# LayerNorm + causal attention + ternary FFN on eight cores: one constant to another queue, an earlier wait for the constants, and part of a 3.5 MB reload moved from SyncE's queue to GpSimd's

## What is computed

```python
xn = layernorm(x)
q = rope((xn @ wq).reshape(B, S, 16, 128));  k = rope(xn @ wk ...);  v = xn @ wv ...
scores = einsum('bqhd,bkhd->bhqk', q, k) / sqrt(128) + causal
attn = softmax(scores) @ v                       # per head
scale = mean(abs(weight))
w_t = clip(round(weight / (scale + 1e-10)), -1, 1) * scale
y = x + attn.reshape(B, S, 2048) @ wo + (xn @ w_t.T + bias)
```

## Time and profile before

| what | us |
|---|---|
| median of 2 runs | 1839.79 |
| the two runs | 1833.55 and 1846.04 |
| the profiled execution, its own time | 1828.61 |
| span of its slowest core (core 5), first to last instruction | 1827.0 |
| spans of the eight cores | 1808.9 to 1827.0 |
| busy on core 5: TensorE / VectorE / ScalarE / GpSimd | 1524.1 / 762.2 / 477.1 / 101.1 |

### The profile page before, as it was taken

One profiled execution on the slowest core, in us unless ns is written; L12 is line 12 of the kernel. 1 busy time (PEld: TensorE's weight loads), 2 busy tenths in 40 slices (PEclk: granted clock), 3 DMA queues, 4 the chain that ended last, 5 costly groups with the idle time before them and its releaser, 6 DMA issues. The chain is left out here.

```text
span 1827.0 us, 29591 instructions; the slowest of 8 cores (1808.9 to 1827.0 us)
## 1 busy us (share of the span) xinstructions
PE 1524.1 (83%) x9096; PEld 879.1 (48%) x9096; DVE 762.2 (42%) x1559; ACT 477.1 (26%) x837; POOL 101.1 (6%) x118
## 2 busy tenths in 40 slices
PE   0505248999999989999999999999938999999999
PEld 0202113444444434444444344444417888888888
DVE  3425254345445365474474564643502222222222
ACT  1000014554454523514524434335230000000000
POOL 1100001011011100000000000000000000000000
PEclk9957579999999999999999999999978999999999
DMA  9993835064364474735835725420065686786772
GB/s 178 151 138 54 90 76 110 27 113 91 98 113 85 87 131 83 135 71 86 133 72 94 135 68 76 75 33 7 12 147 117 164 189 149 177 165 133 162 154 87
DMA packets 350420, 194.93 MB, mean 107 GB/s; under 512 B 240193, under 2 KB 338498, under 8 KB 343874
## 3 DMA queue, kind: packets, MB, share of 16 engines
q0 software_dynamic: 139072, 92.29, 30.3%
q1 hardware_dynamic: 157730, 63.53, 19.5%
q10 hardware_dynamic: 53472, 37.23, 7.0%
HBM read 177.28 MB, written 32.51 MB: 115 GB/s over the span
## 5 line engine op out<-in xcount | busy, mean ns | idle before, releaser
L606 ACT ACTIVATE et<-pC,bias 128x512 bf16<-128x512 f32 (+3 forms) x240 | 149.8, 624 | 626.7 <-PE pC L593 625.7
L500 PE MATMUL pA<-xnT,wslk 128*128 128x512 bf16 x480 | 118.8, 404 | 171.7 <-DMA xnT<-xnn 171.6
L643 PE MATMUL pF<-et,onms 128*128 128x512 bf16 (+3 forms) x640 | 224.5, 352 | 16.1 <-ACT et L606 11.5
L617 DVE TENSOR_TENSOR et<-et,trim 128x128 bf16<-128x128 bf16 x256 | 57.5, 225 | 272.3 <-ACT et L606 268.3
L500 PEld LDWEIGHTS pA<-xnT,wslk 128*128 128x128 bf16 x480 | 47.4, 102 | 232.1 <-issue 187.4
L645 PE MATMUL pG<-et,vh 128*128 128x512 bf16 (+3 forms) x384 | 137.0, 360 | 0.0
L960 PE MATMUL pA<-wtc,xnT 128*128 128x256 bf16 x1024 | 123.9, 275 | 12.2 <-DMA wtc<-wtT_scr 12.2
L606 ACT ACTIVATE et<-pD,bias 128x512 bf16<-128x512 f32 (+3 forms) x208 | 130.7, 628 | 2.7 <-PE pD L593 2.2
L593 PE MATMUL pC<-qTh,kTh 128*128 128x512 bf16 (+3 forms) x240 | 83.9, 350 | 56.3 <-ACT et L606 56.3
L976 PE MATMUL pA<-woc,oTh 128*128 128x256 bf16 x896 | 109.7, 275 | 20.1 <-DMA oTh<-outT_scr 20.1
L960 PE MATMUL pB<-wtc,xnT 128*128 128x256 bf16 x1024 | 123.1, 274 | 0.0
(11 more groups left out here) (99 smaller groups left out, 1852.4 us busy)
## 6 DMA issues: line engine op xcount, KB each, us to landing
xst<-wf POOLq DMA_DIRECT2D x32, 1024.0 KB, 6.5
xst<-x POOLq DMA_DIRECT2D x16, 1024.0 KB, 17.6
xsl<-x SPq DMA_DIRECT2D x128, 128.0 KB, 3.4
wtc<-wtT_scr ACTq DMA_DIRECT2D x16, 1024.0 KB, 11.6
woc<-wo POOLq DMA_DIRECT2D x16, 1024.0 KB, 13.2
y<-osl ACTq DMA_DIRECT2D x128, 128.0 KB, 3.2
wslq<-wq POOLq DMA_DIRECT2D x16, 512.0 KB, 7.7
wslk<-wk POOLq DMA_DIRECT2D x16, 512.0 KB, 9.5
```

The costliest lines, as they stand in the source:

```text
L500: e.matmul(pp[:, 0:CW], wsl[:, it * 128:(it + 1) * 128], bass.AP(xnT, it * S + c * CW, [[NT * S, 128], [1, CW]]), start=(it == 0), stop=False)
L606: e.activation(out=et[slot][:, col0:CW], in_=pc_[:, col0:CW], func=AF.Exp, scale=INV_SQRT_D, bias=bias3[:, :]).then_inc(sems["ac"], 1)
L617: e.tensor_tensor(out=et[slot][:, col0:col0 + 128], in0=et[slot][:, col0:col0 + 128], in1=tri[:, :], op=ALU.mult).then_inc(sems["dv"], 1)
L643: e.matmul(pF[:, col0:CW], onm[:, :], et[slot][:, col0:CW], start=(kt == 0), stop=(kt == nkt - 1))
```

## The change

1. The load of `onr` moves from GpSimd (semaphore `bias`) to SyncE (semaphore `c`), in sixth place of now eight constants. GpSimd's first list has one transfer less.
2. TensorE waits for `c` ahead of its first bias matmul (L177) too, which now reads a tile of that semaphore.
3. VectorE's wait for `c` moves from behind the first LayerNorm tiles to the top of its program, behind two memsets.
4. Of the 14 slices of `oTh[0]`, SyncE keeps ten, on two semaphores in turn (two under way, where there were four). The other four (slices 10 to 13) go to GpSimd on two other semaphores, and they stand between woc 0 and woc 1. Slices 12 and 13 wait for 10 and 11, and woc 1 stands behind them.

```diff
         for dst, src in [(c2, c2_d), (s2, s2_d), (tri, tri_d), (onc, onc_d),
-                         (oncf, oncf_d), (onrf, onrf_d), (onm, onm_d)]:
+                         (oncf, oncf_d), (onr, onr_d), (onrf, onrf_d), (onm, onm_d)]:
             dma("sync", "c", (lambda dst=dst, src=src: (dst[:, :], src, False)),
                 ordered=False)
         consts_c = cnt["c"]
-        dma("gpsimd", "bias", (lambda: (biasb[:, :], bias_d, False)),
-            ordered=False)
-        dma("gpsimd", "bias", (lambda: (onr[:, :], onr_d, False)),
-            ordered=False)
+        dma("gpsimd", "bias", (lambda: (biasb[:, :], bias_d, False)))
...
             e.memset(bias3[:, :], -3.0)
+            e.wait_ge(sems["c"], consts_c)
...
                 if j == 0:
+                    e.wait_ge(sems["c"], consts_c)
                     e.wait_ge(sems["bias"], bv)
...
-        @on("vector")
-        def _(e, cc=consts_c):
-            e.wait_ge(sems["c"], cc)
...
             plan_ph2_weights(0)
+        if do_ph2:
+            for hh in range(10, H - 2):
+                dma("gpsimd", OTH0[2 + (hh % 2)],
+                    (lambda hh=hh: (
+                        bass.AP(oTh[0], hh * 1024, [[H * 1024, 128], [1, 1024]]),
+                        bass.AP(outT_d.tensor, hh * 128 * S, [[S, 128], [1, 1024]]),
+                        False)),
+                    extra_waits=(ph2_finals if hh < 12 else []))
+        if chunks:
             plan_ph2_weights(1)
...
-            for hh in range(H - 2):
-                dma("sync", OTH0[hh % 4],
+            for hh in range(10):
+                dma("sync", OTH0[hh % 2],
...
-                    extra_waits=(ph2_finals if hh < 4 else []))
+                    extra_waits=(ph2_finals if hh < 2 else []))
```

## The result

The changed kernel is slower by 0.86%: ratio to the kernel before 1.0086, 95% interval 1.0059 to 1.0112. On the 1836.66 us median of the kernel before that is +15.8 us (10.8 to 20.6). The median after is 1854.82 us, the profiled execution took 1845.49. The forecast was +8.6 us, within 2%, in a range of 1833 to 1857 us. The direction and the range held; the size was put at about half. In some executions one half of the chip runs at a lower granted clock and all times are longer; the ratios and means here leave those out, the two medians count them.

What follows compares the result with a forecast made beforehand. TensorE, busy 83% of the span, was taken as the bound, so edits act only where it waits. Start +7.1 and phase 2 +1.5 give +8.6 us on the 1836.1 mean: 1844.7, rounded to 1845 us; range 1833 to 1857.

Steps and rivals of the forecast that it cites:

- The start: At the start, VectorE's early wait for the constants delays its first statistics, the first projection and the end by 7.1 us.
- The rival that the wait is hidden by DMA work: At the start, the wait costs nothing, leaving only phase 2's +1.5 us: 1838 us, no measurable change; chance 0.1.
- The other edits at the start: At the start, moving onr's load and TensorE's bias matmuls costs 0 us; bounds -0.5 and 0 for the load.
- The cover that the prediction named: At the start, ScalarE's bias copies stand behind tile 0's 1/sqrt, itself 7.1 us later, giving 4 us of cover.
- Phase 2: At phase 2's beginning, GpSimd's four slices end at 1377 us, later than SyncE's, and set the first woc matmul: +1.5 us.
- The relief for woc 0: In phase 2, fewer SyncE slices under way let woc 0 land 2 us earlier, at about 1369 us; bounds 0 and 3.2.
- SyncE's rounds: In phase 2, ten slices, two under way, take five rounds: 8 + 4 x 5.4 = 29.6 us, ending at 1375.0 us.
- the sum of the wrong side (+1.8): In phase 2, GpSimd's slices put the first woc matmul at 1377 + 0.3 against 1375.5 us; +1.5 was taken.
- Its figure of about -3 us for core 1: In phase 2 on core 1, where woc 0 lands 10.8 us ahead of the matmul, GpSimd's sum gives about -3 us.
- the slices get woc 1's bandwidth: In phase 2, total transfer work binds, so the first woc matmul comes 6.5 us earlier; net +0.6 us, 1837; chance 0.2.
- The third rival: In phase 2, GpSimd's slices take 7.9 + 6 us behind woc 0: matmul +9.5 us, total +16.6, 1853 us; chance 0.15.

Runs made afterwards that it cites:

- e1: The changed kernel with the old phase 2, so only the start edits; ratio to the kernel before 1.0065, mean core span +11.7 us.
- e3: The kernel before with only VectorE's wait for the constants moved to the top; ratio 1.0050, mean core span +7.5 us.
- e5: The changed kernel with SyncE's ten slices on four semaphores, four under way instead of two; ratio to the kernel before 1.0058, mean core span +7.9 us.
- e2: The kernel before with only the phase 2 edits; ratio 1.0031, mean core span +3.1 us.
- e4: The changed kernel with VectorE's wait put back behind the first LayerNorm tiles; ratio to the kernel before 1.0046, mean core span +7.0 us.
- e6: The kernel before with SyncE's 14 slices on two semaphores, two under way instead of four; ratio 1.0033, mean core span +8.2 us.
- e7: The kernel before with all 14 slices under way at once; ratio 1.0009, mean core span -0.8 us.
- e8: The changed kernel with six small constants on their own semaphore, awaited by VectorE only at the old place; ratio to the kernel before 1.0036, span +8.2 us.
- v1: The kernel before with all 14 slices under way and woc 1 and wtc 1 held until they landed; ratio 0.9986, mean core span -8.4 us.
- v2: The kernel before with the two rope tables issued only after x tile 0 landed, on their own semaphore; ratio 0.9986, mean core span -0.7 us.

## Why the prediction was right, and where not

**The start: right, in mechanism and size.** The step was 22.08 - 14.98 = 7.1 us at VectorE, at the first projection and at the end. VectorE begins at 21.7 us on average (forecast 22.1), the first transpose is issued at 28.1 (28.5), the first projection comes at 63.8 us in the four executions with the early wait (after, e1, e3, e5) and at 56.7 in the seven with the wait late and the tables in their old place (before, e2, e4, e6, e7, e8, v1): 7.1 us. The wait alone costs +7.5 ± 1.2. The rival that the wait is hidden by DMA work is out: the DMA share is 0.00 for 6 us.

**The other edits at the start: put at 0, measured about +4.** The prediction bounded moving `onr` and TensorE's wait by -0.5 and 0. The pairs e1 and e3, e4 and e2 say +4.2 ± 1.8 and +3.9 ± 1.5, and e8 against e2, with nearly the same edits, +5.1 ± 1.5 (not independent of the second pair, since e2 is in both). The cover that the prediction named, ScalarE's copies behind tile 0's 1/sqrt, holds in the changed kernel. In e4, where it is gone, the copies do wait, and the 1/sqrt of tile 1 comes right behind them on core 1:

```profile
23.33 0.60 ACT L186 ACTIVATE biasbc<-pH 128x512 bf16<-128x512 f32 x1 [2.57 <-PE pH L175]
24.78 0.62 ACT L201 ACTIVATE biasbc<-pH 128x512 bf16<-128x512 f32 x1
25.26 0.32 ACT L249 ACTIVATE rstd<-mv,epsv 128x1 f32<-128x1 f32 x1
```

That costs VectorE's L267 of tile 1 0 to 1.0 us by core, not 4 us, and nothing at the first projection (56.5 us). The time from the first projection to the last LayerNorm tile (L267) points further: 200.2, 201.9, 201.5, 202.0 and 195.5 us with these edits (after, e1, e4, e8, e5), and 194.2, 199.3, 196.4, 199.5 and 200.2 without (before, e2, e3, e6, e7). The means are 2.3 us apart, but the groups overlap.

The granted clock bears on this. The stretch from the first projection to woc 0's issue took 1261 to 1299 us on the 112 profiled cores (14 executions of eight), and it goes with the time that TensorE's clock stood at the lower of its two levels in it, 133 to 178 us: 0.84 us longer per us, correlation 0.95. Taken from the granted clocks of whole executions (twice the missing share of the clock, times the span), that time is 4.6 ± 2.7 us longer in e1 than in e3, 1.8 ± 1.5 in e4 than in e2 and 2.7 ± 1.1 in e8 than in e2. At the 0.7 us per us by which the executions of the kernel before differ, 1 to 3 of the 4 us would go with the clock (an estimate). Whether the edits bring the lower clock about, or it differed by chance, is not shown. Where these 4 us arise, and whether the queue of `onr` or TensorE's wait makes them, stays open; no run separates the two. If they are real, this is the larger term that was missing from the sum, with the next.

**Phase 2: put at +1.5, measured +2.5 ± 1.0 at the mark and +3.1 ± 1.1 in the span; the binding part was named wrongly.** The prediction let GpSimd's slices set the first woc matmul and SyncE's end 2 us earlier. It was the other way round, by two mis-sized terms:

- The relief for woc 0 was put at 2 us (bounds 0 and 3.2). woc 0 lands 21.3 us after its issue on average, against 27.6 before: 6 us. e6, with two instead of four slices under way and woc 1 still right behind woc 0, has the same relief (21.2), so that the depth of SyncE's queue makes it, and more of it than the work of the missing slices suggested. GpSimd's last slice is therefore done at +27 to +32 us, not at +33.6.
- SyncE's rounds were put at 8 + 4 x 5.4 = 29.6 us. The means over the eight cores are 8.3, 7.2, 6.2, 5.0 and 6.7, sum 33.4. The price of 5.4 came from the last round of core 5, before the end of which woc 0 and wtc 1 had landed (at 1370.9 and 1373.1); over all eight cores that round averages 6.6 us already. After the change the second and third rounds ran with all three queues full, and the last one ran beside woc 1, which GpSimd had just issued. The first round was right.

The term came near all the same, by luck: the sum of the wrong side (+1.8) and the truth (about +3) lie close. The core used also mattered: the prediction went by core 5, the slowest of one execution, and which core is slowest changes from run to run. (Its figure of about -3 us for core 1 is a slip: the same sum, 1360.2 - 2 + 2.5 + 5.5 + 0.3 = 1366.5 against 1371.0, gives -4.5.)

**The whole.** So one of the three terms was right (7.1 against +7.5), one was put at 0 and measured about +4, and one had the wrong mechanism and half the size. That the time lies in the range owes something to its width: the range also took in the 17 us by which executions differ, and the median after is 2 us below its end.

**The rivals.** That the slices get woc 1's bandwidth and the first woc matmul comes 6.5 us earlier did not happen in the changed kernel, although GpSimd issues woc 1 only at +23 to +28 us: SyncE's rounds are one after the other and still run then. v1 shows that the idea is sound if all slices are under way and woc 1 and wtc 1 both wait: 25.3 us, where its expectation's sum by the queues' shares had 21. The third rival, GpSimd's slices as the new wait in full, is out. The rule of the Trainium skill that a DMA has a fixed part ("DMA: Bandwidth & Descriptors", "Anatomy of one DMA") is stated there for transfers that GpSimd issues; the rounds here are SyncE's. e6 agrees in kind: rounds of two slices cost some 3 us even with little else under way, and 5 to 8 in company. Two slices at the 381 GB/s of the earlier trace rows would be 1.4 us, which leaves 1.6 us of such a round (an estimate).

## What to carry to other kernels

A wait moved to the top of an engine's program costs the difference between its own release and the one that it stands ahead of. If that engine feeds the queue that issues the next loads, the DMA engines go empty, and here nothing made it good. Read the release of a semaphore as that of its last transfer, however small, and look at what stands ahead of it in its own queue: issued ahead of the tables, the small constants were in by 7 us. (A kernel with the early wait and that order was not run.) In a stretch bound by transfers, count rounds, price a round in the company it will have, and put what is needed later behind a wait. Four of 14 slices on another queue with two instead of four under way cost about 3 us; all 14 under way with two loads held back that weren't needed yet gave 8 us.

## What the hardware showed

- The last of the small constants (0.2 to 32 KB) landed at 21 to 23 us, though all were issued by 6.3 us. The two 1 MB tables ahead of them in the same queue had landed by 13.9 us (e8), and the three 1 MB loads of x in the other queue by 23 us. Where the small ones stand ahead of the tables (v2), they had landed by 7 us on all cores, beside the same loads of x. So it was what stood ahead in their own queue that held them up.
- Two 256 KB slices in a round took 5.0 to 8.3 us beside two other busy queues, some 3 us with little beside them (e6); four slices took 7.2 to 10.5 us (means over eight cores of the kernel before). So a slice is far from having a fixed price.
- woc 0 landed 21.2 us after its issue with two slices of the other queue under way (e6) and 27.6 with four (before), with nothing else changed: the depth of one queue sets the pace of another. With fourteen (e7) it was 28.1, hardly more than with four; other kernels with four under way had 24.5 (e5) to 27.3.
- The same kernel's executions differ by the time at the lower of the two clock levels: about 0.7 us of mean span per us among 84 executions of the kernel before. On core 3 of the changed kernel the granted clock is 0.50 while TensorE waits from 1353 us on, still 0.50 from 1390 to 1396 after the first woc matmul at 1390.79, and 0.98 from 1396 to 1404.
